# Attention: where ScalarE takes a batch's square root, and which queue stores the heads

## The reference, cut to what matters

```python
def _L1_conv_ref(x, Wq, Wk, Wv, conv_w, proj_w, proj_b):     # HEADS, DIM_HEAD = 8, 16
    q = xs @ Wq.T;  k = xs @ Wk.T;  v = xs @ Wv.T;  v = v + v
    ...                                                       # reshaped to b, n, HEADS, DIM_HEAD
    q = _l2norm(q);  k = _l2norm(k);  v_h = _l2norm(v)
    attn_head = softmax(einsum('bnhd,bngd->bnhg', v_h, v_h), axis=-1)
    q = einsum('bnhg,bngd->bnhd', attn_head, q)
    k = einsum('bnhg,bngd->bnhd', attn_head, k)
    attn = softmax(einsum('bnhd,bnhe->bnde', k, q), axis=-1)
    out = einsum('bnhd,bnde->bnhe', v, attn)                  # then proj_w, proj_b
x = x + _L0_conv_ref(_gn(x), ...)
x = x + _L1_conv_ref(_gn(x), ...)                             # x: 8 x 56 x 56 x 128
```

## Time and profile before

| | us |
|---|---|
| Median of 3 runs | 3128.38 (3125.18 to 3130.5) |
| The profiled execution | 3134.22 |
| Its span, first to last instruction | 3132.4 |
| PE matmul busy | 2862.5 (91%) |
| DVE busy | 1933.0 (62%) |
| ACT busy | 1262.5 (40%) |
| POOL busy | 843.7 (27%) |

### The profile page before, as it was taken

One profiled execution on the slowest core, in us unless ns is written; L12 is line 12 of the kernel. 1 busy time (PEld: TensorE's weight loads), 2 busy tenths in 40 slices (PEclk: granted clock), 3 DMA queues, 4 the chain that ended last, 5 costly groups with the idle time before them and its releaser, 6 DMA issues. The chain is left out here.

```text
span 3132.4 us, 145347 instructions
## 1 busy us (share of the span) xinstructions
PE 2862.5 (91%) x62769; PEld 2113.4 (67%) x62769; DVE 1933.0 (62%) x3276; ACT 1262.5 (40%) x2841; POOL 843.7 (27%) x921
## 2 busy tenths in 40 slices
PE   5778798999999999999999979679999999999889
PEld 4555248966666666666666634348888888888779
DVE  4444353366666666666666657557778887778533
ACT  3555344332222222222222244356666666666300
POOL 0000002012222222222222212225555555555410
PEclk9778698999999999999999999889999999999999
DMA  5778100012112111212121199546666667666556
GB/s 139 213 211 231 53 1 1 0 31 46 45 44 46 44 46 44 46 44 46 44 46 44 43 366 400 228 80 104 106 102 99 100 105 107 102 103 98 80 142 199
DMA packets 839362, 315.48 MB, mean 101 GB/s; under 512 B 671729, under 2 KB 824878, under 8 KB 835118
## 3 DMA queue, kind: packets, MB, share of 16 engines
q1 hardware_dynamic: 503186, 176.24, 23.9%
q10 hardware_dynamic: 321692, 130.88, 15.8%
q0 software_dynamic: 14336, 6.45, 3.7%
HBM read 157.66 MB, written 155.75 MB: 100 GB/s over the span
## 5 line engine op out<-in xcount | busy, mean ns | idle before, releaser
L845 DVE TENSOR_TENSOR terms<-spec,ps_z 112x456 f32<-112x456 f32 x1024 | 575.0, 623 | 404.3 <-PE ps_z L728 404.3
L738 PEld LDWEIGHTS ps_q<-inv_w,prod 112*57 112x57 f32 x16384 | 450.9, 133 | 174.5 <-issue 172.2
L826 POOL TENSOR_TENSOR prod<-terms 112x456 f32<-112x456 f32 x256 | 297.6, 1162 | 1000.5 <-DVE terms L845 1000.5
L738 PE MATMUL ps_q<-inv_w,prod 112*57 112x56 f32 x16384 | 484.4, 217 | 1.2 <-DVE prod L851 1.2
L783 ACT ACTIVATE q_half<-ps_q 121x448 f32<-121x448 f32 x255 | 139.2, 546 | 827.1 <-PE ps_y L746 827.1
L728 PE MATMUL ps_z<-x_half,fwd_w 120*112 120x456 f32 x1024 | 458.4, 570 | 0.0
L1135 POOL TENSOR_TENSOR k_blocks<-k_mixed,same_of 128x896 f32<-128x896 f32 x112 | 188.1, 1680 | 398.2 <-ACT k_mixed L1301 398.2
L1152 POOL DMA_DIRECT2D v_blocks<-v_heads x448 | 272.7, 615 | 41.7 <-PE ps_o L1222 23.5
L728 PEld LDWEIGHTS ps_z<-x_half,fwd_w 120*112 120x112 f32 x1024 | 160.4, 176 | 122.0 <-issue 106.1
L1222 PE MATMUL ps_o<-p_norm,v_blocks 128*64 128x64 f32 x6272 | 213.4, 227 | 26.5 <-DVE p_norm L1386 23.6
L1222 PEld LDWEIGHTS ps_o<-p_norm,v_blocks 128*64 128x64 f32 x6272 | 197.4, 141 | 36.0 <-DVE p_norm L1386 29.8
(11 more groups left out here) (136 smaller groups left out, 4505.7 us busy)
## 6 DMA issues: line engine op xcount, KB each, us to landing
qk_heads<-st_qk ACTq DMA_DIRECT2D x56, 476.0 KB
qk_rows<-qk_heads SPq DMA_DIRECT2D x112, 238.0 KB
conv_in<-v_sb ACTq DMA_DIRECT2D x112, 224.0 KB, 3.3
v_in<-conv_in SPq DMA_DIRECT2D x512, 49.0 KB
conv_out<-y_sb ACTq DMA_DIRECT2D x512, 49.0 KB
y<-conv_out SPq DMA_DIRECT2D x8, 1792.0 KB, 13.2
x_in<-in_x SPq DMA_DIRECT2D x8, 1568.0 KB, 9.5
shortcut<-short ACTq DMA_DIRECT2D x8, 1568.0 KB, 6.2
```

The source lines that it names most:

```text
L738: last = pe.matmul(ps_q[64 * ri:64 * ri + NF, c * SIDE:(c + 1) * SIDE], prod[b % 2][:, x, c * NF:(c + 1) * NF], k.inv_w[:, x, ri * SIDE:(r ...
L826: pool.tensor_tensor(prod[b % 2][:, 1, :], terms[b % 2][:, 2, :], terms[b % 2][:, 3, :], ALU.add).then_inc(prod_i_r, 1)
L845: last = dve.tensor_tensor(terms[b % 2][:, x, :], k.spec[0:NFFT, s, bass.ds(c * CC, CC), :].rearrange("p c f -> p (c f)"), ps_z[b % 2][z][ ...
```

## The change

In ACT's program the root moves from behind leave_mix to directly behind exp_l; store_heads leaves ACT's program. It goes to SP's, with the same waits and the same two DMAs: in the loop store_heads(u//2 + 2) stands ahead of turn(u) for each odd u from 3 on, and ahead of the loop the stores of batches 0, 1 and 2 stand behind load_xn of units 3, 5 and 7.

```diff
@@ SP's program
+            def store_heads(n):
+                at = slice(n * BPB * TB, (n + 1) * BPB * TB)
+                sp.wait_ge(st_r, n + 1)
+                sp.wait_ge(vn_r, n + 1)
+                sp.dma_start(t.VT[at].rearrange("(j p) x -> p j x", p=TB), st_v[n % 2][:]).then_inc(st_stored[n % 2], 16)
+                sp.dma_start(t.QK[at].rearrange("(j p) h x -> p j (h x)", p=TB), st_qk[n % 2][:].rearrange("p j h x -> p j (h x)")).then_inc(st_stored[n % 2], 16)
+
             for w in range(AU + 1):
                 load_xn(w)
+                if w in (3, 5, 7):
+                    store_heads(w // 2 - 1)
             for u in range(NU):
+                if u % 2 and u // 2 + AHEAD - 2 >= AHEAD - 1 and u // 2 + AHEAD - 2 < NB:
+                    store_heads(u // 2 + AHEAD - 2)
                 turn(u)
                 load_xn(u + AU + 1)
@@ ACT's program
-            def store_heads(n):
...
                     if bk // BPB + 1 < AHEAD:
                         root(bk // BPB)
-                    if bk // BPB:
-                        store_heads(bk // BPB - 1)
             for i in range(NU + 1):
                 if unit(i):
                     exp_s(i)
                 if unit(i - 1):
                     exp_l(i - 1)
+                if i % 2 == 0 and i // 2 + AHEAD - 1 < NB:
+                    root(i // 2 + AHEAD - 1)
                 if unit(i + AU):
                     copy_in(2 * (i + AU))
                 if unit(i):
                     leave_mix(i)
-                if i % 2 == 0 and i and i // 2 + AHEAD - 2 < NB:
-                    store_heads(i // 2 + AHEAD - 2)
-                if i % 2 == 0 and i // 2 + AHEAD - 1 < NB:
-                    root(i // 2 + AHEAD - 1)
                 if unit(i + AU):
                     copy_in(2 * (i + AU) + 1)
```

## The result

The changed kernel takes 3259.97 us (median of 4 runs, 3258.93 to 3270.48) against 3127.45 us before: a ratio of 1.043, 95% interval 1.0412 to 1.0449. The forecast was 3235 us, in 3155 to 3305. The profiled execution took 3270.48 us, its span 3268.7; against the one before (3134.22) that is 136 us more.

A forecast was written before the change was run, and what follows sets the result against it. TensorE (PE) was taken to set the pace in attention. Pairs going from 16.25 to 17.9 us add 86 us over 52 pairs, and 21 us come ahead of the loop: 3235 us against the median, range 3155 to 3305.

The forecast's parts named there:

- The root: Attention loop, ScalarE's order: moving the root ends PE's two odd-unit waits, a gain of 0.8 us a pair.
- a cover of 0.5 us for k_blocks: Even unit: k_blocks comes later but still 0.5 us before PE wants it, so this costs nothing.
- The wait on SP: Loop, odd units: the store ahead of the loads in SP's queue makes PE wait 2.45 us a pair.
- The slack: Odd unit's loads: they land 0.75 us before PE wants them, which absorbs part of the 2.45 us delay.
- the bytes: Store's bytes ahead of the odd unit's loads in SP's queue: 0.75 us a pair, bounds 0 and 2.5.
- Ahead of the loop: Before the loop: stores of the first batches delay loads and first scores, +21 us, bounds 8 and 28.
- The 2 to 3 us that ScalarE was to give back: Ahead of the loop: ScalarE no longer waits for st_v, cutting the 24 us delay to 21.
- the third rival: TensorE's clock in the loop: falls to 0.83 in a third of the pairs, +55, 3290 us and up; chance 0.11.
- a falling clock as a sign against it: Profile after: clock expected at 1.00; the forecast is wrong if the clock falls.
- The loads don't feel the store: First rival, loop: loads absorb the delay, pairs take 15.45 us, total 3096 us; chance 0.07.
- The wait just pays for the gain: Second rival, loop: a wait of 0.8 to 1.27 us a pair, total about 3150 us; chance 0.10.

The follow-up runs named there:

- e1: Kernel before with only the root moved behind exp_l, both stores staying in ScalarE's queue: 3085.89 us, ratio 0.9859.
- e2: Changed kernel with the root back in its old place behind leave_mix, stores still in SyncE's queue: 3265.21 us, ratio 1.044.
- e4: e1 plus SyncE waiting for st_v and the norm's copy ahead of each odd unit's loads, issuing no store there: 3118.35 us, ratio 0.9966.
- e6: Changed kernel with the whole store issued a second time, to tensors nothing reads: 3520.56 us, ratio 1.1283.
- e5: Changed kernel with two more small DMAs behind each store in SyncE's queue, to tensors nothing reads: 3400.73 us, ratio 1.0896.
- e7: e1 with only the stores of batches 0 to 2, ahead of the loop, moved to SyncE's queue: 3110.43 us, ratio 0.9955.
- e10: e9 with three added matmuls on PE ahead of each odd unit's scores in the loop: 3426.8 us, ratio 1.0963.
- e3: Changed kernel with the loop's store directly behind the odd unit's loads instead of ahead of them: 3107.24 us, ratio 0.9934.
- e9: Changed kernel with PE's hardware loop written as six units a turn instead of three, as control: 3401.89 us, ratio 1.0877.

## Why the prediction was right, and where it was off

**The root.** Forecast 0.8 us a pair and a cover of 0.5 us for k_blocks in the even unit. e1: 0.81 us a pair, a cover of 0.6. Right. That it was added to the wait as a gain of its own was right in the sum, since the pair was built as 15.45 plus the wait; but e2 shows that with the stores in SP's queue the old order would have been as fast.

**The wait on SP.** Forecast: loads 2.5 us behind the outputs, PE waits 2.45 us. Measured: 2.61 and 2.36. That the two agree so well is in part luck, as errors in the parts made up for each other. The slack is 1.1 us (e4) instead of 0.75: the loads land 6.6 us behind their first issue as before, but PE wants them 7.7 us behind the outputs' end and not 7.47. By the changed kernel against e4, issues and bytes together add 2.36 - 0.53 = 1.83 us: the loads start 0.96 us later, and the rest, 0.9 us (0.84 by the timelines), is the bytes, for which I had taken 0.75. So about a third of the 2.8 us of the store's bytes counts. The reason that I gave for counting only a part, that the loads' issues run on while the bytes ahead drain, did not hold: the issues themselves are held up, 3.35 us for four instead of 2.56, and that is where the bytes cost. The rule of the Trainium skill that the choice of the issuing engine only saves issue time (DMA: Bandwidth & Descriptors, "Issuing engines are not separate DMA queues") would have left out the bytes; e6 against e5, with 1.95 us for 672 KB, and the 2.62 us of SP's issues beside a store from ACT's queue, go with the order in a ring that the same page has under "Queues, rings and completion order".

**Ahead of the loop.** Forecast 21 us, measured 24.5 (e7 less e1; 21.4 and 27.8 within one group of runs). The first scores were forecast 24 us later and come 24.7 later in the trace. The 2 to 3 us that ScalarE was to give back are seen in no run.

**The clock.** This term was missing in the forecast, and had stood as the third rival with a chance of 0.11. The prediction named 1.00 as the clock to expect and a falling clock as a sign against it, and that sign came: 0.96 in 2200 to 2800 us. So the forecast is right in the wait and in the place ahead of the loop, and incomplete behind the wait. A pair of 15.45 and a wait of 2.36 gives 17.8; the trace has 18.5. The rest, 0.7 us, is 53 x 0.7 = 37 us, more than the 25 by which the median lies above the forecast. It comes as 1.5 us in 15 of 33 pairs, which is 0.7 a pair. PE's busy time a pair says the same: 525.1/32.5 = 16.2 us in the changed kernel, 599.9/39 = 15.4 in e1, with the same matmuls. The same remainder grows where the granted clock is lower: e4, 15.45 + 0.53 = 16.0 against 16.0 measured (75 units in 600 us), clock 1.00; the changed kernel 0.7 at 0.96; e5, 15.45 + 4.01 = 19.5 against 21.4 (56 units), 1.9 at 0.90; e6, 15.45 + 5.96 = 21.4 against 24.0 (50 units), 2.6 at 0.86. That the stretched matmuls are the remainder is read off the traces. That filling the wait brings some of it back is seen in PE's busy time in e10, beside a disturbed control; that it would save time is not shown.

The sum, with measured terms: 53 x (-0.81 + 2.36 + 0.7) = 119, and 24.5 ahead of the loop: 144 us, for 136 between the two profiled executions and 133 between the medians. With 53 pairs in place of 52 the forecast itself would have been 2 us higher.

**The rivals.** "The loads don't feel the store" is out by e4, e5 and e6. "The wait just pays for the gain" comes near e4 (0.53 us of wait, 10 us under the kernel before), not the change. The third rival came true in a smaller size beside the forecast.

## What to carry to other kernels

A DMA that is moved to another engine's queue brings its waits and its bytes along, and everything behind it in that queue inherits them: ask what is queued behind, when its consumer wants it, and put the moved issue behind the transfers that are due first. Behind the loads the same store costs nothing (e3), ahead of them 153 us. Where the engine that sets the pace gets a wait of some microseconds a turn, look also at what its clock does behind it.

## What was not expected of the hardware

- SP itself is held up when bytes stand ahead in its queue: the four v_blocks issues take 2.56 us with nothing ahead and 2.62 us beside a store from ACT's queue, but 3.35 us behind the store in the same queue, 3.56 in e5 and 4.85 behind twice the bytes in e6 (means). Behind the loads, the store's first issue takes 1.36 us in e3 instead of 0.32.
- Small DMAs were not cheaper to issue. The two extra ones of e5, of 448 pieces of 32 bytes, take 0.53 and 0.77 us (medians). The two in the same place of e6, with 448 pieces of 512 and of 1088 bytes, take 0.53 and 0.97. The store's own two, ahead of them and with the same pieces as those of e6, take 0.32 and 0.50; what makes them shorter is not shown.
- Idle time of 2.69 us on PE was followed by scores and logits of 2.35 and 2.86 us instead of 1.80 to 1.85 and 1.86. Of 33 waits 15 were followed by such a stretch, none of them under 2.26 us; one of 2.77 us was not.
- The same matmuls on PE in a loop of six units a turn instead of three take 142 us longer (e9 against the changed kernel), with 140 packets of an instruction queue in 600 us where there were none.
